# One gated cross-attention block with a mixture of experts: an expert product in front of the score maxima, stack copies in front of a scaling, loads with semaphores of their own, and the division of the expert weights moved into the first step

## The chip, the core and the metric

The kernel runs on 1 core of a Trainium2 chip. The core has a matrix engine (PE in the profile, with its weight loads as PEld), a vector engine (DVE), an activation engine (ACT), GpSimd (POOL) and a queue engine (SP) that issues the transfers between the chip's memory and the core's. The engines work through instruction lists of their own, each in order, and wait for each other by semaphores. The metric is the device time of one execution in microseconds. A step in this text is one pass of the kernel's outer loop, numbered from 0.

## The reference, cut to what matters

There are 32 rows (batch entries) of 256 tokens with 256 features, and for each row 77 context tokens with 192 features. A block of attention with 16 heads of 16 features and a two-layer product behind it is added to x through a gate, and then a mixture of 8 experts, of which 2 count for each token, through another.

```python
x = x + tanh(g_xattn) * xattn(layernorm(x), ctx)     # q, k, v with biases, softmax, relu(out @ W1 + b1) @ W2 + b2
x = x + tanh(g_ffn) * ffn(layernorm(x))

def ffn(x):                                          # E = 8 experts, K = 2
    scores = maximum(x @ gate_W + gate_b, 1e-4)
    p = softmax(scores)
    w = maximum(p, 0.1) at the top 2, divided by its sum; 0 elsewhere
    y = einsum('bsd,edf->bsef', x, expert_W) + expert_b
    return einsum('bsef,bse->bsf', y, w) / 2
```

## The kernel before

All weights stay in the core. Nearly every product is made three times, as high and low halves: a matrix is rounded to a high part (`we_hi`, `wkv_hi`, `w1_hi`, ...), usually by ACT, and what the rounding lost is the low part (`we_lo`, ...), usually made by DVE; PE then adds low x high, high x low and high x high. The expert weights are kept in float16 and are first divided by a power of two near their largest magnitude: DVE reduces `we_f` to `w_amax`, PE transposes it, DVE makes the power, PE spreads it over the partitions (`power_spread`), DVE makes `w_scale`, ACT makes `we_hi` (`experts_high`) and DVE `we_lo` (`experts_low`, four parts and a fifth piece for the gate weights and expert biases).

The outer loop is written by hand as a pipeline over rows: step s holds the front of row s (norm, keys, values, queries, score maxima, stacks), the middle of row s - 1 (`scores`, exponentials `exps`, `attend`, the two-layer product, second norm), the first experts of row s - 2 and the last experts of row s - 3. There are 35 steps; rows 0 to 31 have their front in steps 0 to 31. Each engine has its own `step` function, and the order of the calls there is the order of its instructions. Nothing reorders them.

Places that the change and the prediction touch:

- The maxima: `scores_for_max(b, i)` (line 845) are six products of the queries with `k_block`, a block form of the keys that POOL makes in two halves (`key_blocks(b, 0)` and `(b, 1)`, line 426). Product 0 waits for the first half, product 1 for the second. Between the halves POOL does `stack_comb` (three kinds of small copies). DVE reduces each product (`take_max`).
- The experts: `experts(e, eu, i, ...)` is one product of six matmuls of 512 columns (line 711, tile `e`), in two PSUM banks in turn. Products 2 and 3 are scaled by ACT (`scale_expert`, line 621), the other six are scaled and added by DVE (line 1156).
- The query stacks: PE transposes `q_stack` in two halves (line 911), ACT copies them (`qs_copy_a`, `qs_copy_b`, lines 602 and 606). The next step's `transposes_x` (line 720) writes the bank that `qs_copy_b` reads. ACT then goes on with `x2T_high` (612), `xnT_high` (522) and the first exponentials (544, 545); DVE makes `p_lo` from these (1139) and PE's first `attend` (780) reads it.
- The start: SP issues all transfers; nine of them share the semaphore `first_loaded`, which ACT and DVE await in whole. ACT runs `experts_high` in step 1, between its stack copies and `oT_high` (line 582), for whose low half `oT_lo` PE's `mlp_up` waits. DVE runs `experts_low` in step 1, among the maxima and `h_low` (line 1234, for `mlp_down`, line 894) and ahead of the second norm (`xn`, line 1254, for line 921).

Of the kernel before, what the change touches and what calls it, by code (L numbers as in the profile page):

```python
# [16 lines left out]
F32 = mybir.dt.float32  # L17
# [3 lines left out]
ALU = mybir.AluOpType  # L21
# [40 lines left out]
def gated_block(nc, x, y, g_xattn, g_ffn, Wq, bq, Wk, bk, Wv, bv, W1, b1, W2, b2,  # L62
# [5 lines left out]
    with ExitStack() as ctx:  # L68
# [29 lines left out]
        w_amax, w_top, w_power = sb("w_amax", [P, 2]), sb("w_top", [2, 1]), sb("w_power", [2, 1])  # L98
# [73 lines left out]
        first_loaded = sem("first_loaded")  # L172
        w_loaded = sem("w_loaded")
        we_loaded = sem("we_loaded")
# [4 lines left out]
        tanh_ready, b2g_ready = sem("tanh_ready"), sem("b2g_ready")  # L179
# [44 lines left out]
        FIRST, WEIGHTS = 9, 8  # L224
# [44 lines left out]
        def _(sp):  # L269
# [22 lines left out]
            for dst, src in [(wq_f[:], Wq.rearrange("(k p) n -> p k n", p=P)),  # L292
                             (wkv_f[:, :, 0:D], Wk.rearrange("(k p) n -> p k n", p=YC)),
                             (wkv_f[:, :, D:2 * D], Wv.rearrange("(k p) n -> p k n", p=YC)),
                             (bq_rows[:], bq.partition_broadcast(P)),
                             (bkv_rows[:, 0:D], bk.partition_broadcast(M)),
                             (bkv_rows[:, D:2 * D], bv.partition_broadcast(M)),
                             (gates[:, 0:1], g_xattn.partition_broadcast(P)),
                             (gates[:, 1:2], g_ffn.partition_broadcast(P)),
                             (b2_rows[:], b2.partition_broadcast(P))]:  # L300
                sp.dma_start(dst, src).then_inc(first_loaded, 16)
            sp.wait_ge(consts_ready, EARLY)
            for dst, src in [(w1_f[:], W1.rearrange("(k p) n -> p k n", p=P)),
                             (w2_f[:], W2.rearrange("(k p) n -> p k n", p=P)),
                             (gb_rows[:], gate_b.partition_broadcast(P)),
                             (gw_f[:], gate_W.rearrange("(k p) n -> p k n", p=P)),
# [5 lines left out]
            load(0, 1, 1)  # L312
            for k in range(KC):
                sp.dma_start(we_f[:, k, :].rearrange("p (e f) -> p e f", e=E),
                             expert_W[:, k * P:(k + 1) * P, :].rearrange("e p f -> p e f")).then_inc(we_loaded, 16)
# [6 lines left out]
        def _(pool):  # L322
# [121 lines left out]
            pool.wait_ge(b2g_ready, 1)  # L444
            x_with_bias(0, 0)

            def step(pair, u, s):
# [21 lines left out]
                if has(s, 0):  # L469
                    q_low(b)  # L470
                    v_parts(b, u)
                if has(s, 1) and s > 0:
                    first_norm_scale(n)
# [994 lines left out]
```

## Time and profile before

| what | value |
|---|---|
| time, median of 3 runs | 1013.13 us (1012.97 to 1013.41) |
| the profiled execution's own time | 1012.68 us |
| its span, first to last instruction | 1011.0 us |
| PE busy | 945.1 us, 93% |
| DVE, ACT, POOL busy | 82%, 71%, 64% |
| steps 0, 1 and 2 begin with line 720 at | 7.0, 34.6 and 75.4 us |
| a step in the middle | 29.5 us |

PE is busy nearly all the time from step 3 on; the profile's share counts overlapping ends of matmuls, so small waits show as less idle time than they cost. The first three steps are less dense. A row's start, its duration, the engine, the line and the tiles are read from left to right; what stands in square brackets is how long the engine was idle before it and what ended that.

### The profile page before, as it was taken

To read this page: it belongs to the slowest core of one execution; us is meant where nothing else is said; L and a number is where in the kernel's file an instruction comes from. 1 tells how busy PE (TensorE), PEld (TensorE's weight loads), DVE (VectorE), ACT (ScalarE), POOL (GpSimd) and SP (SyncE) were. 2 spreads that over 40 slices of the span, in tenths; PEclk is the share of its full clock that TensorE was granted. 3 is DMA by queue.
4 is the path that set the end of the run, shared out by engine and by line. 5 is a ranking of instruction groups with operands and counts; after the bars stand their busy time and mean duration, and the time that the engine had idled before them with its cause. 6 is when DMAs were issued, how large, how long until landed. Compare 5 with 4: busy or idle time off the path is not lost.

```text
span 1011.0 us, 26189 instructions
## 1 busy us (share of the span) xinstructions
PE 945.1 (93%) x9410; PEld 692.7 (69%) x9410; DVE 824.9 (82%) x2134; ACT 721.1 (71%) x1517; POOL 651.8 (64%) x856
## 2 busy tenths in 40 slices
PE   2758999999999999999999999999999999999997
PEld 2546677777767777776777777677777777777763
DVE  3566888888888888888888888888888888888875
ACT  4556787777778777777877777787777778777661
POOL 4435566777666677766667776666777666677643
PEclk9977999999999999999999999999999999999999
DMA  6000000000000000000000000000000000000000
GB/s 207 14 11 4 15 24 25 25 22 15 25 15 25 24 25 22 15 25 15 25 24 25 22 15 24 14 25 25 25 23 15 25 14 25 25 12 11 12 13 21
DMA packets 17472, 24.62 MB, mean 24 GB/s; under 512 B 2798, under 2 KB 8896, under 8 KB 17344
## 3 DMA queue, kind: packets, MB, share of 16 engines
q1 hardware_dynamic: 17344, 22.94, 7.1%
q8 instruction: 77, 1.26, 0.5%
q14 instruction: 51, 0.42, 0.1%
HBM read 14.54 MB, written 8.39 MB: 23 GB/s over the span
## 4 chain that ended last, share of the span: by engine, by line
PE 68%; POOL 11%; ACT 9%; issue 7%; DVE 3%; DMA 1%; SPq 0%; POOLq 0%; DVEq 0%; ACTq 0%
PE e L711 21%; PE g L711 20%; PE t L894 9%; POOL p_lo L372 6%; POOL k_block L426 5%; PE t L760 5%; PE s L845 4%; ACT qsT L606 3%; ACT scaled L621 2%; PE g L720 2%; ACT p_hi L545 2%; PE s L780 1%; PE g L856 1%; PE s L781 1%; PE s L782 1%
## 5 line engine op out<-in xcount | busy, mean ns | idle before, releaser
L372 POOL TENSOR_TENSOR p_lo<-p_f,p_hi 77x512 f16<-77x512 f32 x160 | 183.2, 1161 | 234.3 <-ACT p_hi L545 234.3
L711 PE MATMUL e<-we_hi,x2T_lo 128*128 128x512 f16 x496 | 188.9, 381 | 0.0
L711 PE MATMUL e<-we_hi,x2T_hi 128*128 128x512 f16 x496 | 188.4, 380 | 0.0
L711 PE MATMUL e<-we_lo,x2T_hi 128*128 128x512 f16 x496 | 188.4, 380 | 0.0
L544 ACT ACTIVATE p_f<-t 77x512 f32<-77x512 f32 x256 | 151.9, 593 | 24.8 <-PE t L760 24.4
L1156 DVE SCALAR_TENSOR_TENSOR acc<-e,comb,acc 128x256 f32<-128x256 f32 x307 | 145.9, 475 | 14.1 <-PE e L711 11.8
L545 ACT ACTIVATE p_hi<-t 77x512 f16<-77x512 f32 x256 | 151.9, 593 | 0.0
L1201 DVE TENSOR_REDUCE row_max<-s 128x6 f32<-128x462 f32 (+1 forms) x192 | 108.0, 576 | 11.4 <-PE s L845 11.4
L780 PEld LDWEIGHTS s<-v_hi,p_lo 77*128 77x128 f16 x1024 | 83.3, 96 | 32.2 <-issue 19.5
L780 PE MATMUL s<-v_hi,p_lo 77*128 77x17 f16 x1024 | 97.8, 172 | 5.2 <-POOL p_lo L372 2.5
L426 POOL TENSOR_TENSOR k_block<-own_head,khT 128x616 f16<-128x616 f16 x64 | 95.1, 1488 | 5.7 <-ACT khT L575 5.7
L621 ACT ACTIVATE scaled<-e,comb 128x256 f32<-128x256 f32 x126 | 53.0, 472 | 61.8 <-PE e L711 61.8
L782 PE MATMUL s<-v_hi,p_hi 77*128 77x17 f16 x1024 | 96.4, 170 | 0.0
L781 PE MATMUL s<-v_lo,p_hi 77*128 77x17 f16 x1024 | 96.3, 171 | 0.0
L760 PE MATMUL t<-qsT,kz 128*77 128x256 f16 x512 | 91.6, 282 | 2.8 <-ACT p_hi L545 2.5
L711 PEld LDWEIGHTS e<-we_hi,x2T_hi 128*128 128x128 f16 x496 | 48.5, 98 | 58.9 <-issue 0.6
L781 PEld LDWEIGHTS s<-v_lo,p_hi 77*128 77x128 f16 x1024 | 82.4, 96 | 7.1
L711 PE MATMUL g<-oT_hi,w_lo 128*128 128x256 f32 x256 | 80.8, 316 | 4.0 <-DVE oT_lo L1227 4.0
L845 PE MATMUL s<-k_block,qhT 128*128 128x308 f16 (+2 forms) x256 | 67.2, 307 | 16.4 <-POOL k_block L426 14.5
L590 ACT ACTIVATE h_hi<-g,b_cols 128x256 fp32r<-128x256 f32 x128 | 60.9, 476 | 29.4 <-PE g L711 27.6
L782 PEld LDWEIGHTS s<-v_hi,p_hi 77*128 77x128 f16 x1024 | 81.5, 96 | 0.0
L1139 DVE TENSOR_TENSOR p_lo<-p_f,p_hi 77x512 f16<-77x512 f32 x96 | 69.5, 724 | 13.6 <-ACT p_hi L545 13.6
(189 smaller groups left out, 2924.0 us busy)
## 6 DMA issues: line engine op xcount, KB each, us to landing
x_sb<-in_x SPq DMA_DIRECT2D x32, 256.0 KB, 2.6
out<-acc SPq DMA_DIRECT2D x32, 256.0 KB, 2.0
we_f<-in_L_ffn_expert_W SPq DMA_DIRECT2D x2, 1024.0 KB, 9.2
y_sb<-in_ctx SPq DMA_DIRECT2D x32, 57.8 KB
w_f<-in_L_xattn_W SPq DMA_DIRECT2D x2, 512.0 KB
wq_f<-in_L_xattn_Wq SPq DMA_DIRECT2D x1, 256.0 KB
wkv_f<-in_L_xattn_Wk SPq DMA_DIRECT2D x1, 192.0 KB
wkv_f<-in_L_xattn_Wv SPq DMA_DIRECT2D x1, 192.0 KB
```

The costliest lines, as they stand in the source:

```text
L372: pool.tensor_tensor(p_lo[:, r].rearrange("m h n -> m (h n)"), p_f[:, r, :], p_hi[:, r].rearrange("m h n -> m (h n)"), ALU.subtract).then_ ...
L426: pool.tensor_tensor(k_block[:, c * PAIRS:(c + 1) * PAIRS, :], own_head[:], khT[:, c, :].unsqueeze(1).to_broadcast([P, PAIRS, M]), ALU.mul ...
L544: act.activation(p_f[:, r, :], TT[g % 2][0:M, :], ACT.Exp, scale=SCALE).then_inc(exps_done, 1)
L545: act.activation(p_hi[:, r].rearrange("m h n -> m (h n)"), TT[g % 2][0:M, :], ACT.Exp, scale=SCALE).then_inc(exps_done, 1)
L711: mm = pe.matmul(out_ap, a, c, start=(i == 0), stop=(i == n - 1))
L760: mm = pe.matmul(TT[g % 2][0:M, e * N:(e + 1) * N], kz[:, g, e, :], qsT[:, g, :], start=True, stop=True)
L780: pe.matmul(dst, lo, v_hi[:, u, h, :], start=True, stop=False)
L781: pe.matmul(dst, hi, v_lo[:, u, h, :], start=False, stop=False)
L782: mm = pe.matmul(dst, hi, v_hi[:, u, h, :], start=False, stop=True)
L845: mm = pe.matmul(S[i % 2][:, at * M:(at + n) * M], qhT[:, h // PAIRS, t * P:(t + 1) * P], k_block[:, h:h + n, :], start=True, stop=True)
L1156: dve.scalar_tensor_tensor(out=acc[:, u, t, :], in0=BANK[product_banks(r)[i]][:, j * D:(j + 1) * D], scalar=comb[:, u, t, 2 * c + j:2 * c ...
L1201: dve.tensor_reduce(row_max[:, t, h:h + n], S[i % 2][:, 0:n * M].rearrange("p (h m) -> p h m", h=n), AX.X, ALU.max).then_inc(max_taken, 1)
```

## The change

1. PE: `experts(e, eu, 0, ...)` stands in front of `scores_for_max(b, 0)` instead of behind it (30 steps, 2 to 31, have both).
2. ACT: `qs_copy_a` and `qs_copy_b` stand in front of the second `scale_expert` (product 3) instead of behind it (the same 30 steps).
3. SP: the loads come in another order and with own semaphores: keys and values first, then the query weights, biases, the second row, the gates, the 2 MB of expert weights, and only then the two-layer weights. ACT and DVE wait for what they read.
4. The division of the expert weights is moved from steps 0 and 1 into step 0: the reduction is split over the two loads, the transposes, the power and the scales stand between the keys and the maxima of row 0, `experts_high` (ACT) and the first `experts_low` (DVE) end in step 0, and the other four pieces of `experts_low` are spread over step 1. The rounding of the two-layer weights goes to the end of step 0.

```diff
@@ SP @@
-            for dst, src in [(wq_f[:], ...), (wkv_f[:, :, 0:D], ...), (wkv_f[:, :, D:2 * D], ...), (bq_rows[:], ...),
...
-                sp.dma_start(dst, src).then_inc(first_loaded, 16)
+            sp.dma_start(wkv_f[:, :, 0:D], Wk.rearrange("(k p) n -> p k n", p=YC)).then_inc(kv_loaded, 16)
+            sp.dma_start(wkv_f[:, :, D:2 * D], Wv.rearrange("(k p) n -> p k n", p=YC)).then_inc(kv_loaded, 16)
+            sp.dma_start(wq_f[:], Wq.rearrange("(k p) n -> p k n", p=P)).then_inc(wq_loaded, 16)
...
+            load(0, 1, 1)
+            sp.dma_start(gates[:, 0:1], g_xattn.partition_broadcast(P)).then_inc(gates_loaded, 16)
+            sp.dma_start(gates[:, 1:2], g_ffn.partition_broadcast(P)).then_inc(gates_loaded, 16)
+            for k in range(KC):
+                sp.dma_start(we_f[:, k, :].rearrange("p (e f) -> p e f", e=E),
+                             expert_W[:, k * P:(k + 1) * P, :].rearrange("e p f -> p e f")).then_inc(we_loaded[k], 16)
             sp.wait_ge(consts_ready, EARLY)
+            sp.dma_start(gw_f[:], gate_W.rearrange("(k p) n -> p k n", p=P)).then_inc(gw_loaded, 16)
             for dst, src in [(w1_f[:], W1.rearrange("(k p) n -> p k n", p=P)),
                              (w2_f[:], W2.rearrange("(k p) n -> p k n", p=P)),
...
@@ ACT @@
-            act.wait_ge(first_loaded, 16 * FIRST)
-            act.activation(tanh_g[:], gates[:], ACT.Tanh).then_inc(tanh_ready, 1)
-            for hi, full in ((wkv_hi, wkv_f), (wq_hi, wq_f)):
-                act.activation(hi[:], full[:], ACT.Copy).then_inc(w_hi_ready, 1)
+            act.wait_ge(kv_loaded, 32)
+            act.activation(wkv_hi[:], wkv_f[:], ACT.Copy).then_inc(w_hi_ready, 1)
...
                     highT_copies(b)
                     q_stack_high(b)
                     k_stack_high(b)
-                if s == 1:
-                    experts_high()
+                if s == 0:
+                    weights_high()
+                    experts_high((0, 1))
...
                 if front:
                     kz_copy(b)
+                if s == 0:
+                    experts_high((2, 3))
+                    gate_and_biases_high()
...
-                if first:
-                    scale_expert(e, eu, 3, s - 2)
                 if front:
                     qs_copy_a(b)
                     qs_copy_b(b)
+                if first:
+                    scale_expert(e, eu, 3, s - 2)
                 if mid:
                     x2T_high(m, mu)
@@ PE @@
-                if s == 1:
-                    largest_weight_transposed()
...
-                if s == 1:
-                    power_spread()
...
+                if first:
+                    experts(e, eu, 0, s - 2)
+                if s == 0:
+                    largest_weight_transposed()
                 if front:
                     scores_for_max(b, 0)
-                if first:
-                    experts(e, eu, 0, s - 2)
+                if s == 0:
+                    power_spread()
@@ DVE @@
                 if front:
                     q_high(b)
                 if s == 0:
-                    weights_low()
+                    largest_expert_weights(0)
+                    largest_expert_weights(1)
+                    largest_weights()
+                    gate_factors()
+                    power_of_largest()
+                if s == 1:
+                    experts_low(2)
...
+                if s == 0:
+                    weight_scales()
                 if front:
                     take_max(b, 1)
                     take_max(b, 2)
                     kz_copy(b)
-                if s == 1:
-                    experts_low(0)
...
-                if s == 1:
-                    experts_low(2)
...
                 if s == 1:
-                    experts_low(3)
                     experts_low(PARTS)
...
                 if s == 0:
-                    largest_weights()
+                    weights_low()
+                    experts_low(0)
```

On PE, at the place in a middle step where the last of the products of `p` with the values (`s1<-v_hi,p_hi`) gives way to the maxima of the next row, this stood before (the line numbers of the two kernels differ; the three rows of tile e0, the expert product, stand twice in a row and are shown once):

```order
L782 MATMUL s1<-v_hi,p_hi 128x17
L845 MATMUL s0<-k_block,qhT 128x462
L711 MATMUL e0<-we_hi,x2T_lo 128x512
L711 MATMUL e0<-we_lo,x2T_hi 128x512
L711 MATMUL e0<-we_hi,x2T_hi 128x512
L856 MATMUL g0<-ident32,o 128x128 x4
L790 MATMUL g1<-ident32,comb_stack 96x128 x2
L845 MATMUL s1<-k_block,qhT 128x154
```

and this stands there now:

```order
L802 MATMUL s1<-v_hi,p_hi 128x17
L731 MATMUL e0<-we_hi,x2T_lo 128x512
L731 MATMUL e0<-we_lo,x2T_hi 128x512
L731 MATMUL e0<-we_hi,x2T_hi 128x512
L865 MATMUL s0<-k_block,qhT 128x462
L876 MATMUL g0<-ident32,o 128x128 x4
L810 MATMUL g1<-ident32,comb_stack 96x128 x2
L865 MATMUL s1<-k_block,qhT 128x154
```

The six expert matmuls and the first product with `k_block` changed places; from the output transposes (`g0<-ident32,o`) on, to the first product with the second half of `k_block` (128x154), the order is as before.

On ACT, at the end of a middle step, this stood before:

```order
L490 ACTIVATE xn<-x_sb,neg_mean 128x256 x2
L494 ACTIVATE xn<-xn,rstd 128x256 x2
L621 ACTIVATE scaled<-e,comb 128x256 x2
L602 ACTIVATE qsT<-g 128x1024
L606 ACTIVATE qsT<-g 128x1024
L612 ACTIVATE x2T_hi<-g 128x512
L522 ACTIVATE xnT_hi<-g 128x512
```

and this stands there now:

```order
L492 ACTIVATE xn<-x_sb,neg_mean 128x256 x2
L496 ACTIVATE xn<-xn,rstd 128x256 x2
L612 ACTIVATE qsT<-g 128x1024
L616 ACTIVATE qsT<-g 128x1024
L631 ACTIVATE scaled<-e,comb 128x256 x2
L622 ACTIVATE x2T_hi<-g 128x512
L532 ACTIVATE xnT_hi<-g 128x512
```

The two scalings moved behind the two stack copies, and stand now between these and the copies that open the next step (`x2T_hi`, `xnT_hi`).

On ACT in the first two steps, the part of step 0 behind the key stack reads now as follows (before, `kz` followed `k_stack` directly, `w_hi` stood ahead of the second row's norm, and `we_hi`, `gw_hi` and `eb_stack` stood in step 1 ahead of `oT_hi`):

```order
L568 ACTIVATE k_stack<-k_hi 77x32x16
L514 ACTIVATE w_hi<-w_f 128x1024 x2
L520 ACTIVATE we_hi<-we_f,w_scale 128x2x512 x2
L608 ACTIVATE kz<-t 64x8x77
L520 ACTIVATE we_hi<-we_f,w_scale 128x2x512 x2
L524 ACTIVATE gw_hi<-gw_f,w_scale 128x16
L527 ACTIVATE eb_stack<-eb_f,w_scale 32x256 x2
L612 ACTIVATE qsT<-g 128x1024
```

Everything that turns loaded weights into high parts stands now ahead of row 0's stack copies `qsT`, and nothing of it is left in step 1.

## Rows read from the trace of the kernel before

**Rows 1.** PE's waits: us in total, times, the longest in us

```profile
PE s L845 <- POOL k_block L426: 14.5, 31, 2.7
PE g L720 <- ACT qsT L606: 7.8, 30, 1.3
```

**Rows 2.** Step 2 and a middle step: stretch, length, busy PE PEld DVE ACT POOL, PEclk, DMA

```profile
75.40:109.20 33.80, 30.71 (x278) 22.11 (x276) 22.26 (x60) 22.27 (x48) 16.03 (x23) 0.83 0.04 10
404.00:433.40 29.40, 28.76 (x294) 21.16 (x295) 25.08 (x67) 22.14 (x48) 20.17 (x26) 1.00 0.07 22
```

**Rows 3.** Timeline of a middle step around the maxima; start, duration, engine

```profile
417.13 0.35 PE L845 MATMUL s<-k_block,qhT 128*128 128x462 f16 x1 [0.38 <-POOL k_block L426]
...
419.27 0.36 PE L845 MATMUL s<-k_block,qhT 128*128 128x154 f16 x2
...
415.33 1.70 POOL L426 TENSOR_TENSOR k_block<-own_head,khT 128x616 f16<-128x616 f16 x1
...
417.81 1.26 POOL L426 TENSOR_TENSOR k_block<-own_head,khT 128x616 f16<-128x616 f16 x1
...
415.11 0.80 DVE L1139 TENSOR_TENSOR p_lo<-p_f,p_hi 77x512 f16<-77x512 f32 x1
```

**Rows 4.** Timeline of that step's end and the next one's start, PE and ACT

```profile
430.41 1.06 PE L911 MATMUL g<-ident,q_stack 128*128 128x128 f16 x16
...
433.43 0.63 PE L720 MATMUL g<-ident,xn 128*128 128x128 f32 x4 [0.22 <-ACT qsT L606]
...
436.52 0.17 PE L780 MATMUL s<-v_hi,p_lo 77*128 77x17 f16 x1
...
430.62 0.84 ACT L621 ACTIVATE scaled<-e,comb 128x256 f32<-128x256 f32 x2 [1.88 <-PE e L711]
431.34 1.02 ACT L602 ACTIVATE qsT<-g 128x1024 f16<-128x1024 f16 x1
432.25 1.03 ACT L606 ACTIVATE qsT<-g 128x1024 f16<-128x1024 f16 x1
433.24 0.60 ACT L612 ACTIVATE x2T_hi<-g 128x512 f16<-128x512 f32 x1
434.09 0.60 ACT L522 ACTIVATE xnT_hi<-g 128x512 fp32r<-128x512 f32 x1 [0.25 <-PE g L720]
```

**Rows 5.** Timeline of step 0, and the start of step 1 (the last row)

```profile
10.80 0.20 ACT L499 ACTIVATE tanh_g<-gates 128x2 f32<-128x2 f32 x1 [3.91 <-DMA b_rows<-in_L_xattn_b]
...
15.54 0.68 PE L711 MATMUL g<-wkv_hi,yT_lo 96*77 96x512 f32 x1 [7.16 <-DVE yT_lo L1133]
...
21.67 0.43 DVE L1176 CAST q_hi<-q 128x512 f16<-128x512 f32 x1
...
34.58 1.09 PE L720 MATMUL g<-ident,xn 128*128 128x128 f32 x4 [1.27 <-ACT qsT L606]
```

**Rows 6.** The tile we_f: count, ns min/median/max, first and last start in us

```profile
L512 ACT ACTIVATE we_hi<-we_f,w_scale x4: 1164/1171/1179, 51.3 to 54.4; 128x1024 f16<-128x1024 f32 x4
L1123 DVE SCALAR_TENSOR_TENSOR we_lo<-we_f,w_scale,we_hi x4: 1275/1280/2377, 59.5 to 69.2; 128x1024 f16<-128x1024 f32 x4
L314 SPq DMA_DIRECT2D we_f<-in_L_ffn_expert_W x2: 373/1074/1774, 11.4 to 11.8; - x2
L1088 DVE TENSOR_REDUCE w_amax<-we_f x1: 4412/4412/4412, 31.0 to 31.0; 128x1 f32<-128x4096 f32 x1
...
DMA to landing us min/median/max: 8.0/9.2/10.4
```

**Rows 7.** Timeline of step 1 where PE waits for ACT or DVE

```profile
56.72 0.60 ACT L582 ACTIVATE oT_hi<-g 128x512 fp32r<-128x512 f32 x1
...
58.09 0.58 PE L711 MATMUL g<-oT_hi,w_lo 128*128 128x256 f32 x1 [4.04 <-DVE oT_lo L1227]
...
67.69 0.38 PE L894 MATMUL t<-w_hi,h_lo 128*128 128x256 f32 x1 [2.01 <-DVE h_lo L1234]
...
73.91 0.66 PE L921 MATMUL g<-ident,xn 128*128 128x128 f32 x2 [3.25 <-DVE xn L1254]
```

More of the change, by code:

```diff
@@ L97, in gated_block @@
         gb_rows = sb("gb_rows", [P, E])
-        w_amax, w_top, w_power = sb("w_amax", [P, 2]), sb("w_top", [2, 1]), sb("w_power", [2, 1])
+        w_amax, w_top, w_power = sb("w_amax", [P, 3]), sb("w_top", [2, 1]), sb("w_power", [2, 1])
         w_spread = sb("w_spread", [2, P])
@@ L496, in _, with query_weights_high, gate_tanh @@
             first_norm(0, 0)
[L498 to L501 removed]
+            act.wait_ge(kv_loaded, 32)
+            act.activation(wkv_hi[:], wkv_f[:], ACT.Copy).then_inc(w_hi_ready, 1)
+            def query_weights_high():
+                act.wait_ge(wq_loaded, 16)
+                act.activation(wq_hi[:], wq_f[:], ACT.Copy).then_inc(w_hi_ready, 1)
+            def gate_tanh():
+                act.wait_ge(gates_loaded, 32)
+                act.activation(tanh_g[:], gates[:], ACT.Tanh).then_inc(tanh_ready, 1)
             def weights_high():
@@ L506, in weights_high, with experts_high @@
                     act.activation(hi[:], full[:], ACT.Copy).then_inc(w_hi_ready, 1)
-            def experts_high():
+            def experts_high(parts):
                 act.wait_ge(w_scale_done, 1)
-                for i in range(PARTS):
+                for i in parts:
                     cols = slice(i * E * D // PARTS, (i + 1) * E * D // PARTS)
@@ L734, in largest_weight_transposed @@
             def largest_weight_transposed():
-                pe.wait_ge(w_amax_done, 2)
-                pe.transpose(BANK["e0"][0:2, 0:P], w_amax[:], ident32[:]).then_inc(w_amaxT_in_psum, 1)
+                pe.wait_ge(w_amax_done, 4)
+                pe.transpose(BANK["e0"][0:2, 0:P], w_amax[:, 0:2], ident32[:]).then_inc(w_amaxT_in_psum, 1)
             def power_spread():
@@ L1068, in _, with key_value_weights_low, query_weights_low, gate_factors @@
             first_norm_sums(0)
-            dve.wait_ge(first_loaded, 16 * FIRST)
-            dve.wait_ge(tanh_ready, 1)
-            dve.tensor_scalar(b2g_rows[:], b2_rows[:], tanh_g[:, 0:1], None, ALU.mult).then_inc(b2g_ready, 1)
-            dve.tensor_scalar(ffn_scale[:], tanh_g[:, 1:2], 1.0 / TOP_K, None, ALU.mult).then_inc(b2g_ready, 1)
-            for i, (lo, hi, full) in enumerate(((wkv_lo, wkv_hi, wkv_f), (wq_lo, wq_hi, wq_f))):
-                dve.wait_ge(w_hi_ready, i + 1)
-                dve.tensor_tensor(lo[:], full[:], hi[:].bitcast(F32), ALU.subtract).then_inc(w_lo_ready, 1)
-            dve.wait_ge(b2g_ready, 2)
+            def key_value_weights_low():
+                dve.wait_ge(w_hi_ready, 1)
+                dve.tensor_tensor(wkv_lo[:], wkv_f[:], wkv_hi[:].bitcast(F32), ALU.subtract).then_inc(w_lo_ready, 1)
+            def query_weights_low():
+                dve.wait_ge(w_hi_ready, 2)
+                dve.tensor_tensor(wq_lo[:], wq_f[:], wq_hi[:].bitcast(F32), ALU.subtract).then_inc(w_lo_ready, 1)
+                dve.wait_ge(consts_ready, CONSTS)
+                dve.wait_ge(rows_loaded, 48)
+            def gate_factors():
+                dve.wait_ge(tanh_ready, 1)
+                dve.tensor_scalar(ffn_scale[:], tanh_g[:, 1:2], 1.0 / TOP_K, None, ALU.mult).then_inc(ffn_scale_ready, 1)
             def weights_low():
-                dve.wait_ge(consts_ready, CONSTS)
                 dve.wait_ge(w_loaded, 16 * WEIGHTS)
+                dve.tensor_scalar(b2g_rows[:], b2_rows[:], tanh_g[:, 0:1], None, ALU.mult).then_inc(b2g_ready, 1)
                 for i, (lo, hi, full) in enumerate(((w1_lo, w1_hi, w1_f), (w2_lo, w2_hi, w2_f))):
```

72 lines of the change are left out of this document (40 added, 32 removed).

## The prediction

> **What bounds the kernel now.** I read the shares by engine, then PE's waits, then single steps. PE sets the pace: its idle time is a few short waits per step. The largest in sum is that of the maxima for `k_block` [rows 1]: 14.5 us over 31 times, 2.7 of them in step 0, so (14.5 - 2.7) / 30 = 0.39 us in each later step. Then comes that of `transposes_x` for the second stack copy, 7.8 us, 1.3 of them at the start of step 1 [rows 1, 5], so (7.8 - 1.3) / 29 = 0.22 us a step. The change stands in front of just these two. A step in the middle lasts 29.4 us from one `transposes_x` to the next, and step 2 lasts 33.8 us at a mean granted clock of 0.83 [rows 2]: it alternates between 1.2 and 2.4 GHz. From step 3 on the clock is up. Steps 0 and 1 are no steady pipeline: step 1 begins at 34.58 us [rows 5], and in it PE idles 4.04, 2.01 and 3.25 us for three products that wait on ACT or DVE [rows 7]. So there are two sums to make: thirty nearly equal steps, and the start.
>
> **Steady steps, the expert product in front of the maxima.** It removes nothing. Six matmuls that stood behind product 0 of the maxima now fill PE's time until the first half of `k_block` is there. That half ends at 415.33 + 1.70 = 417.03 and PE starts 0.10 later, at 417.13 [rows 3]. With the expert product ahead, PE has no wait there. But what is late next is the second half, in the same POOL queue behind `stack_comb`: it ends at 417.81 + 1.26 = 419.07. Product 1 stands behind the same work as before, and started at 419.27 [rows 3], 0.20 after the half was ready; of that 0.10 is the hop just measured. Nothing in the change makes POOL earlier: its chain begins with `khT` and with `p_lo`, which hang on PE's and ACT's earlier part of the step. So product 1 can start at 419.07 + 0.10 = 419.17 at the earliest. The wait of 0.39 us goes from product 0 to product 1, and **0.10 us a step** is left as gain. The output transposes and `oT_low` come earlier by the whole wait, but they are not what PE awaits next. I take 29 steps (3 to 31): -2.9 us. The bounds: 0 if the hop to product 1 is slower by 0.1, and 0.39 x 29 = 11.3 us if POOL does come earlier.
>
> The length of the second half matters, since it now ends the wait. The first half takes 1.70 and the second 1.26 us; beside the first runs DVE's `p_lo`, which itself takes 0.80 [rows 3]. If the second took 1.70 as well, product 1 would start 0.44 later and the step would be 0.44 - 0.10 = 0.34 us longer, not 0.10 shorter; the sum takes 1.26, since POOL does that half at the same time as before and DVE's order beside it is the same but for a shift of some tenths. The Trainium skill, GPSIMD Engine Reference, section 1, says that GpSimd shares its SBUF interfaces with VectorE and contends with DVE instructions that read two SBUF tensors. The trace agrees: the slow half is the one beside `p_lo`, which reads two. By that rule the second half keeps its 1.26, as long as nothing of that kind comes beside it, and the sum is the same.
>
> **Steady steps, the stack copies in front of the scaling.** ACT's order was scaling 430.62, copies 431.34 and 432.25, `x2T_hi` 433.24, `xnT_hi` 434.09 [rows 4]. The copies can't simply move up by the scaling's 0.72: the first needs eight of the sixteen transposes that begin at 430.41 and take 1.06 [rows 4], so it is ready at about 430.41 + 1.06 / 2 + 0.1 = 431.05. It starts 0.29 earlier, the second at 431.96, and, with the old hop of 433.43 - 432.25 - 1.03 = 0.15, PE's `transposes_x` at 431.96 + 1.03 + 0.15 = 433.14 instead of 433.43. But the scaling then stands between the copies and `x2T_hi`: 431.05 + 0.91 + 0.91 = 432.87, two scalings 0.72, `x2T_hi` at 433.6, `xnT_hi` half a microsecond later at 434.1, against 434.09 before. From there ACT goes without a gap to the first exponentials, DVE's `p_lo` and PE's first `attend` at 436.52 [rows 4], and PE waits there for whatever it gained. So the price is **0 to +0.04 us a step**; I take +0.02 x 29 = +0.6 us. Bounds: the 0.22 of [rows 1] in full, -6.4 us, if `attend` does not hang on ACT; and, if the copies came no earlier at all, 0.29 more a step, +8.4. Behind the later scaling wait the bank of product 3 for the last row's product 5, a step later, and POOL's `add_scaled`, later still; both have time.
>
> **Step 0.** ACT stood idle 3.91 us up to 10.80 for the last of nine loads [rows 5], so it was free at 6.89. Keys and values stand now right behind the first row in SP's queue and have a semaphore of their own, and I take them as landed by then. Each microsecond that they were later would be one on this chain. So `wkv_hi` begins 4.0 us earlier, and the low query half no longer stands ahead of the first product: keys start at about 10.9 instead of 15.54, and `q_hi`, which ended at 21.67 + 0.43 = 22.10, ends at about 17.5 [rows 5]. Then come the new parts. The reduction of the expert weights takes 4.41 us [rows 6] in two halves, to about 22. The loads must be there: they were issued at 11.4 and 11.8 and landed 8.0 and 10.4 us later [rows 6], at 19.4 and 22.2, behind 1 MB of other weights; now they are issued about 5 us earlier and ahead of that megabyte, so I put them at 14 to 18, ahead of their halves. Power, spread and scale are ten short instructions on DVE and PE; I bound them by 1.5 and 3 us and take 2.3: scales at 24.3. ACT's block is long: from the first `we_hi` at 51.3 to `oT_hi` at 56.72 it took 5.4 us [rows 6, 7], and with `kz` in it, which I put at 0.7, 6.1; so it ends at about 30.5. In that time lie the six maxima and the stack transposes, which are the cover on DVE and PE. Then come the two copies, 1.02 + 0.91 (as in [rows 4]), and step 1 starts at about 32.6 instead of 34.58 [rows 5]: **-2.0 us**. Ahead of the block ACT rounds the two-layer weights, which are now loaded last. All loads had landed by 11.8 + 10.4 = 22.2 [rows 6], the bytes are the same, and two roundings of about 1.1 us (estimate, from 1.17 for the same shape, [rows 6]) end at 24.4, just when the scales come: no cover is left there, and each microsecond that these loads are later is one on the path. Bounds: -2.8 and +0.5.
>
> **Step 1.** Without ACT's block `oT_hi` comes right behind the output transposes, and of the 4.04 us some 0.35 stay, the time of the copy and its low half: -3.7. `h_lo` was late because a part of `we_lo` stood ahead of it (2.38 us, the longest of the four, [rows 6]); the parts are moved into DVE's idle time earlier in the step, and -2.0 follows [rows 7]. The fourth part (1.28) no longer stands ahead of the second norm, the fifth piece does: -1.2 of the 3.25 [rows 6, 7]. Against that, the moved parts run beside POOL's `p_lo`, and such a part took up to 1.1 us longer than the others [rows 6]: +0.3, bounds 0 and +2.2. Together **-6.6 us** (-7.3 to -4.4).
>
> **Step 2.** It begins with the same idle stretch ahead of it, only shorter, so I expect it to start at 1.2 GHz again; but denser work should bring the clock up a little sooner: **-1.0 us**, bounds 0 and 33.8 - 29.4 = 4.4 [rows 2].
>
> The last three steps are unchanged. The sum: -2.0 - 6.6 - 1.0 - 2.9 + 0.6 = -11.9 us. On the profiled execution's 1012.68 (span 1011.0 and 1.7 around it) that is 1000.8 us; the median of the runs shown is 0.45 above that execution, within the steps' rounding.
>
> **The rivals.**
> *Both steady waits vanish.* Then 0.61 us a step go, 17.7 us, in place of 2.3: 985 us. For it: the rows name just these waits. Against it: the 0.20 us at product 1, and the unbroken ACT chain. 7%.
> *The clock stays up.* If the shorter stalls of step 1 don't let it fall, step 2 takes a middle step's time: another -3.4, 997.4 us. Against it: 2 us of idling are left of the 3.25 ahead of step 2. 12%. The Trainium skill, TensorE: Matmul & The Clock Gate, part 1, says that the throttled state is the default and activity releases it, which speaks for this; the trace agrees, with 0.83 in step 2 and 1.00 in the denser step [rows 2].
> *Loads bind step 0.* If the expert or two-layer weights land 4 to 6 us later than reckoned, the moved division waits in the middle of step 0, ACT with it, and its gain turns to +2 to +4: 1005 to 1007 us. 7%.
> *The second half of `k_block` slows to 1.70.* +0.34 x 29 = +9.9 in place of -2.9: 1013.6, no change. 3%.
> *ACT becomes the bound, slower than before.* If the scaling's whole 0.84 [rows 4] is added between the copies and `xnT_hi`, because the copies wait for the transposes anyway, a step grows by up to 0.84: +24.4 in place of +0.6, 1024.6 us. It decides from (2.0 + 6.6 + 1.0 + 2.9) / 29 = 0.43 us a step on. Against it: the half of the transposes is done 0.29 ahead of the old start of the copies. 4%.
>
> **How the numbers follow.** The forecast case has 67%. I predict 1000.8 us; the range of 993 to 1008 holds it with its unknown costs, the warm step 2 and the late loads, and leaves out the first rival and the last two, 14%, and some tails. Faster by over 0.2% (2 us, about what a measurement here can tell): 93%. Within: 3%. Slower: 4%.
>
> **What would show it.** PE's wait for `k_block` stays near 0.4 us a step, but in front of the 154-column product; a step lasts 29.3 to 29.5 us; `transposes_x` waits less and the first `attend` more. Step 1 begins near 32.6, step 2 near 66 us, and no wait of over 1 us for `oT_lo` or `h_lo` is left. A step under 29 us, or ACT idle while PE waits for `w_amax` or for loads in step 0, would make me wrong.

## The result and the profile after

The changed kernel takes 1005.78 us (median of 4 runs, 1004.77 to 1007.32), the kernel before, run beside it, 1013.05 us: the ratio is 0.993, with a 95% interval of 0.991 to 0.995. The forecast was 1000.8 us in a range of 993 to 1008. The sign and the range held; of the 11.9 us that the sum promised, some 7 came.

The waits of PE after, in us in total, times and longest, answer to [rows 1]:

```profile
PE g L740 <- ACT xn L496: 7.1, 1, 7.1
PE s L865 <- POOL k_block L427: 6.3, 29, 0.2
PE s L800 <- DVE p_lo L1174: 5.0, 4, 4.2
PE e L756 <- DVE w_amax L1123: 4.7, 1, 4.7
PE g L941 <- DVE xn L1289: 2.8, 2, 2.2
PE s L800 <- POOL p_lo L373: 2.7, 5, 0.7
```

The first row is the start of the program. The wait for `k_block` fell from 14.5 to 6.3 us, that of the steady `transposes_x` for `qsT` is gone, as are, in this execution, those for `oT_lo` and `h_lo` of step 1 [rows 7]. A new one came: 4.2 us, once, for DVE's `p_lo`. Next, steps 1, 2 and a middle one (stretch, length, busy PE PEld DVE ACT POOL, PEclk, which is the granted share of TensorE's 2.4 GHz, DMA share and GB/s), to be held against [rows 2]:

```profile
32.40:68.70 36.30, 25.93 (x230) 20.92 (x231) 26.68 (x47) 19.22 (x39) 16.34 (x20) 0.84 0.09 23
68.70:101.90 33.20, 30.96 (x278) 22.96 (x277) 22.06 (x59) 21.58 (x46) 16.00 (x23) 0.81 0.03 11
396.20:425.60 29.40, 29.00 (x295) 21.21 (x294) 25.21 (x67) 21.93 (x48) 20.16 (x26) 1.00 0.08 22
```

The starts of `transposes_x` in the two traces, stretch by stretch, say where the time went:

| stretch | before | after | difference | forecast |
|---|---|---|---|---|
| to step 1 | 34.58 | 32.39 | -2.2 | -2.0 |
| step 1 | 40.85 | 36.32 | -4.5 | -6.6 |
| step 2 | 33.85 | 33.22 | -0.6 | -1.0 |
| steps 3 to 30, each | 29.467 | 29.430 | -0.04, -1.0 in all | -0.08, -2.3 in 29 steps |
| from step 31 to the end | 76.6 | 78.2 | +1.6 | 0 |

The columns add up to -6.8 (spans of 1011.0 and 1004.2 us). Three rows want a cause: step 1, the middle steps, the end.

**Step 1.** The timeline of the changed kernel there, DVE and then POOL (start, duration):

```profile
46.74 5.33 DVE L1174 TENSOR_TENSOR p_lo<-p_f,p_hi 77x512 f16<-77x512 f32 x1 [1.50 <-ACT p_hi L555]
...
44.85 2.51 POOL L373 TENSOR_TENSOR p_lo<-p_f,p_hi 77x512 f16<-77x512 f32 x2 [2.21 <-ACT p_hi L555]
47.33 2.46 POOL L427 TENSOR_TENSOR k_block<-own_head,khT 128x616 f16<-128x616 f16 x2
49.75 0.66 POOL L379 TENSOR_TENSOR k_stack<-kv,k_hi 77x256 f16<-77x256 f32 x1
50.38 1.14 POOL L385 TENSOR_TENSOR q_stack<-q,q_hi 128x512 f16<-128x512 f32 x1
51.47 0.86 POOL L419 CAST v_hi<-kv 77x256 f16<-77x256 f32 x1
```

DVE's difference, 0.80 us in a middle step [rows 3], takes 5.33. It ends at 52.07, 0.60 behind the start of POOL's cast, and that cast takes 0.86 where it takes 0.40 in the trace of before. Until then POOL went from one two-input instruction to the next without a gap. So DVE seems to be let in only where one of POOL's instructions begins, and then that one is held for it.

**The middle steps.** PE's rows around the maxima and ACT's at the step's end, then POOL's second half and DVE's `h_lo`:

```profile
411.65 0.37 PE L865 MATMUL s<-k_block,qhT 128*128 128x154 f16 x2 [0.22 <-POOL k_block L427]
...
422.92 1.06 PE L931 MATMUL g<-ident,q_stack 128*128 128x128 f16 x16
...
425.65 0.63 PE L740 MATMUL g<-ident,xn 128*128 128x128 f32 x4
...
423.57 1.02 ACT L612 ACTIVATE qsT<-g 128x1024 f16<-128x1024 f16 x1 [2.42 <-PE g L931]
424.49 1.02 ACT L616 ACTIVATE qsT<-g 128x1024 f16<-128x1024 f16 x1
425.39 0.84 ACT L631 ACTIVATE scaled<-e,comb 128x256 f32<-128x256 f32 x2
426.11 0.62 ACT L622 ACTIVATE x2T_hi<-g 128x512 f16<-128x512 f32 x1
426.58 0.63 ACT L532 ACTIVATE xnT_hi<-g 128x512 fp32r<-128x512 f32 x1
427.06 0.61 ACT L554 ACTIVATE p_f<-t 77x512 f32<-77x512 f32 x1
...
410.33 1.26 POOL L427 TENSOR_TENSOR k_block<-own_head,khT 128x616 f16<-128x616 f16 x1
...
417.08 1.04 DVE L1269 TENSOR_TENSOR h_lo<-h_f,h_hi 128x256 fp32r<-128x256 f32 x2
```

Count from the query stack's transposes. `transposes_x` follows 425.65 - 422.92 = 2.73 us later, where it was 3.02 [rows 4]: 0.29 won. But `xnT_hi` comes 426.58 - 422.92 = 3.66 later, against 3.68 [rows 4]. The gain is spent inside ACT's queue. At the maxima, the 154-column product starts 411.65 - (410.33 + 1.26) = 0.06 behind the second half of `k_block`, against 0.20 [rows 3]: 0.14 won. Yet from the end of that half to the next query stack transposes it is 422.92 - 411.59 = 11.33 us, and was 430.41 - 419.07 = 11.34 [rows 3, 4]. Two `h_lo` that took 0.95 together in the trace of before take 1.04, `mlp_down` gets its fourth chunk 0.09 later, and the matmuls right behind the wait lose 0.04. So the step looks like a ring, stack transposes, ACT, exponentials, both key halves on POOL, maxima, `h_lo`, `mlp_down` and round again, on which each edit wins at its place and loses the same a little further.

**The end.** Two stretches with the same work, of before (first fence) and after, with the same columns as above:

```profile
963.80:973.80 10.00, 8.54 (x112) 5.34 (x113) 9.10 (x20) 8.69 (x18) 5.88 (x7) 1.00 0.01 2
```

```profile
955.40:965.40 10.00, 8.36 (x89) 4.62 (x89) 8.89 (x21) 8.02 (x18) 5.62 (x5) 0.83 0.01 2
```

In the third step from the end PE has little to do and waits several times for ACT and POOL. There the granted clock stood at 1.2 GHz for about a third of the stretch in the changed kernel, (1 - 0.83) / 0.5, and not in the profiled execution of before. Not all of the 1.6 us is the clock's: 0.27 of it is the mark itself, since with the stack copies in front `transposes_x` of step 31 stands that much earlier against the work of ACT and POOL around it. The table counts the same 0.27 as a gain up to step 3.

### The profile page after: what moved, and what is told of

Same layout as the page of the kernel before. It is cut to its first block, busy times and chain, and to the rows that moved or that the text cites. A ratio compares the mean times of both kernels' runs of the same rounds, so it can differ in the third digit from the quotient of the medians.

```text
span 1004.2 us, 26188 instructions
## 1 busy us (share of the span) xinstructions
PE 952.2 (95%) x9410; PEld 692.0 (69%) x9410; DVE 833.8 (83%) x2136; ACT 714.3 (71%) x1517; POOL 652.1 (65%) x856
## 3 DMA queue, kind: packets, MB, share of 16 engines
q8 instruction: 77, 1.26, 0.5%
## 4 chain that ended last, share of the span: by engine, by line
PE 62%; POOL 16%; ACT 9%; issue 7%; DVE 4%; DMA 1%; SPq 1%; POOLq 0%; ACTq 0%; DVEq 0%
PE g L731 19%; PE e L731 16%; PE t L914 9%; POOL k_block L427 8%; POOL p_lo L373 6%; PE t L780 3%; PE s L865 3%; ACT p_hi L555 3%; PE g L931 2%; DVE p_lo L1174 2%; ACT qsT L616 2%; PE s L800 1%; ACT p_f L554 1%; DMA we_f<-in_L_ffn_expert_W 1%; PE s L801 1%
## 5 line engine op out<-in xcount | busy, mean ns | idle before, releaser
L554 ACT ACTIVATE p_f<-t 77x512 f32<-77x512 f32 x256 | 154.3, 603 | 26.3 <-PE t L780 25.9
L555 ACT ACTIVATE p_hi<-t 77x512 f16<-77x512 f32 x256 | 154.4, 603 | 0.0
L612 ACT ACTIVATE qsT<-g 128x1024 f16<-128x1024 f16 x32 | 32.7, 1023 | 76.0 <-PE g L931 76.0
L1174 DVE TENSOR_TENSOR p_lo<-p_f,p_hi 77x512 f16<-77x512 f32 x96 | 74.6, 777 | 9.3 <-ACT p_hi L555 5.2
L914 PE MATMUL t<-w_hi,h_lo 128*128 128x256 f32 x256 | 78.2, 305 | 0.5 <-issue 0.2
```

The source lines that it names most:

```text
L554: act.activation(p_f[:, r, :], TT[g % 2][0:M, :], ACT.Exp, scale=SCALE).then_inc(exps_done, 1)
L555: act.activation(p_hi[:, r].rearrange("m h n -> m (h n)"), TT[g % 2][0:M, :], ACT.Exp, scale=SCALE).then_inc(exps_done, 1)
L914: mm = pe.matmul(T_DOWN[t][:, 0:D], a[:, c, rows], w[:, c, :], start=(c == 0 and i == 0), stop=(c == HC - 1 and i == 2))
```

## The experiments

"Middle steps" is the mean of steps 3 to 30. Kernels with the same code in those steps differ by 0.02 us in it (29.430 to 29.450), so less than that is not resolved.

**Each steady edit alone,** on the kernel before:

```diff
-                if front:
-                    scores_for_max(b, 0)
                 if first:
                     experts(e, eu, 0, s - 2)
+                if front:
+                    scores_for_max(b, 0)
```

> The kernel before with one edit: TensorE issues the expert product in front of the first maxima product. Theory of a loop (the step is a ring: query_stack_transposes on PE, stack copies and exponentials on ACT, both k_block halves on POOL, maxima, mlp_down, again): PE reaches the 154-column product when the second k_block half lands, which is 0.14 us a step earlier than before, and h_low then runs beside POOL's q_low, is 0.09 us longer, and gives most of it back; the middle steps last 29.45 to 29.47 us (before 29.47), mlp_down starts its fourth chunk 0.09 us late. Rival (the prediction's sum): 0.10 us a step is kept, middle steps of 29.37. Total 1010 to 1013 by the theory, near 1010 by the rival.

```diff
-                if first:
-                    scale_expert(e, eu, 3, s - 2)
                 if front:
                     qs_copy_a(b)
                     qs_copy_b(b)
+                if first:
+                    scale_expert(e, eu, 3, s - 2)
```

> The kernel before with one edit: ACT makes the two stack copies in front of the scaling of expert product 3. Theory of a loop: transposes_x no longer waits for qsT, but x2T_hi, xnT_hi and the exponentials stand behind the scaling, and begin 4.14 us after query_stack_transposes where they began 4.17 after; the middle steps last 29.44 us. Rival (the prediction's sum): 0.00 to 0.04 us longer than before, 29.47 to 29.51. A second rival: the whole wait of 0.22 us of transposes_x is won, 29.25. Total about 1012 by the theory.

Middle steps of 29.463 and 29.454 us against 29.467: neither edit is worth anything that can be seen alone, and the rivals of 29.37 and 29.25 are out. The times, 1014.91 and 1015.43 us in one run each, lie above what was expected, but within the seven runs of the kernel before beside them, 1012.10 to 1015.74. In the first kernel PE's wait for `k_block` fell to 10.0 us, in the second that for `qsT` to 1.3: the waits went, the time stayed. The second kernel had a surprise that was not expected of it. Its start is that of before, and still its `p_low(7)` in step 1 took long:

```profile
48.73 3.35 DVE L1139 TENSOR_TENSOR p_lo<-p_f,p_hi 77x512 f16<-77x512 f32 x1 [2.44 <-ACT p_hi L545]
...
49.07 2.47 POOL L426 TENSOR_TENSOR k_block<-own_head,khT 128x616 f16<-128x616 f16 x2
51.50 1.12 POOL L378 TENSOR_TENSOR k_stack<-kv,k_hi 77x256 f16<-77x256 f32 x1
```

Here it ended at 52.08, 0.58 behind the start of `k_low`, which took 1.12 in place of 0.67. So the stall does not need the new start: the old one can have it too. It came in one of three profiles with the old start, and in all seven with the new one in which POOL was not made to wait for `p_low(7)`.

**The start alone, and the changed kernel again** (the first is the changed kernel with both edits above undone):

> The changed kernel with both steady edits undone (expert product behind the first maxima product, stack copies behind the scaling); the new start stays. Theory: step 1 begins at 32.4 us, lasts 36.3 with p_low(7) at 5.3 us on DVE, step 2 lasts 33.2, middle steps 29.47; 1.0 us above the changed kernel, near 1006.5. Rival (the steady edits are worth the prediction's 2.3 us): near 1008.

> The changed kernel again, as it is. Theory (DVE's two-input difference is held off by back-to-back two-input work of POOL, which the order of the start sets up): p_low(7) of step 1 takes 5.3 us again, PE waits 4.2 us for it, step 1 lasts 36.3. Rival (a chance of one execution): p_low(7) takes about 0.9 us and step 1 lasts 32 to 33, the time is near 1002. The short fall of TensorE's clock in step 32, which one profile of the changed kernel has and that of before has not, comes again if the program sets it, and not always if it is chance (1.3 to 1.7 us).

1005.84 us (ratio 0.992, 0.991 to 0.994) and 1006.34 (0.993, 0.991 to 0.995), run on the same chip: the whole gain that these runs can tell is the start's, and the 1.0 us that was expected between the two did not show. No run separates the start's two parts, the order of the loads and the moved division. Middle steps 29.457 and 29.433. The stall came in both, 4.46 and 4.48 us long, with PE waiting 3.1 us for it. It was shorter than 5.33 because DVE was let in one instruction of POOL earlier: this time `q_low` was the one that was held, 1.60 us in place of 1.15. In the second execution PE also waited 1.1 us for `h_lo` in step 1, which it had not done in the first of the same kernel.

The short fall of the clock near the end came in both as well. The steps there are in the first kernel those of before, and its end takes 77.81 us against 76.61: ACT runs level with the trace of before, to 0.02 us, until 36 us behind the start of step 31, and is 1.21 us late at 43 us; the clock fell at 34.87 and rose at 38.28. So the fall is worth 1.2 us. From step 31 to the end it takes 77.5 to 79.2 us in every other profile of this study, and all but one of them (the keys together, below) have that fall. The execution that the forecast was reckoned from, with 76.6, did not.

**What holds `p_low(7)` up.** First DVE begins it later, by a write to a scratch tile `nap`; then POOL leaves it a gap:

```diff
+                if s == 1:
+                    dve.wait_ge(exps_done, 16)
+                    dve.memset(nap[:], 0.0)
                 if mid:
                     p_low(m, 7)
```

> The changed kernel with one small write of DVE to a scratch tile in step 1, between the end of the exponentials and p_low(7), so that p_low(7) begins about 0.3 us later. Theory (the difference gets in only at the end of one of POOL's two-input instructions, and which one is a matter of phase): p_low(7) lasts about 0.55 us from the start of some POOL instruction on, and that one is 0.46 us longer than usual; a start 0.2 to 0.3 us ahead of the first k_block, as in the middle steps, gives 0.8 to 0.95 us, another phase gives 2 to 5 us. Rival (the length depends on what the start left behind on DVE or on late data): 4.5 to 5.3 us wherever it begins. Step 1 lasts 32.2 to 33 us in the first case, 35.5 to 36.3 in the last.

```diff
+                if s == 1:
+                    pool.wait_ge(p_lo_vector, len(VECTOR_LOW))
                 if has(s, 0):
                     key_blocks(b, 0)
```

> The changed kernel, with one wait more: in step 1 POOL begins the key blocks only when DVE has done p_low(7). Theory (POOL's back-to-back two-input work holds DVE off): p_low(7) ends about 0.55 us after POOL's second p_lo, 1.2 us at most, PE's wait of 3.1 to 4.2 us for it goes, step 1 lasts 32 to 33 us where it lasted 35.5 to 36.3, and the total is 3 to 4 us below the changed kernel, near 1003. Rival (something else is late by then, a load or the second norm): the wait moves, step 1 stays above 35.

The first is inconclusive on the phase: the exponentials ended earlier in that execution, so in spite of the write `p_low(7)` began 0.57 us ahead of the first `k_block`, about as in the first profile of the changed kernel (0.59), lost that start and the next two, and ended 0.58 behind the start of `q_low`, 4.21 us long. With 35.06 us for step 1 it lies between the two that were expected. The second decides. 1000.21 us, step 1 lasts 32.31, step 2 31.61, and the stall is gone (DVE, then POOL):

```profile
45.84 1.43 DVE L1176 TENSOR_TENSOR p_lo<-p_f,p_hi 77x512 f16<-77x512 f32 x1 [1.25 <-ACT p_hi L557]
...
43.94 2.77 POOL L373 TENSOR_TENSOR p_lo<-p_f,p_hi 77x512 f16<-77x512 f32 x2 [1.94 <-ACT p_hi L557]
47.34 2.47 POOL L427 TENSOR_TENSOR k_block<-own_head,khT 128x616 f16<-128x616 f16 x2 [0.63 <-DVE p_lo L1176]
```

DVE gets in at the end of POOL's second `p_lo`, 43.94 + 2.77 = 46.71, and is done 0.56 later. With a wait of 0.6 us on POOL, step 1 is 4.0 us shorter than in the first profile of the changed kernel. Another clock could do that too, but does not here. Steps 1 and 2 of the kernel with the start alone, which stalls (first fence), and of this one, with the columns of the step table:

```profile
32.26:68.47 36.21, 25.68 (x231) 20.78 (x232) 26.68 (x47) 19.22 (x39) 16.20 (x20) 0.71 0.07 20
68.47:101.36 32.89, 29.09 (x279) 21.06 (x277) 23.43 (x60) 22.13 (x48) 15.98 (x23) 0.90 0.04 11
```

```profile
31.76:64.07 32.31, 25.39 (x230) 20.46 (x231) 22.82 (x47) 19.25 (x39) 16.09 (x20) 0.71 0.08 24
64.07:95.68 31.61, 28.47 (x277) 21.52 (x277) 22.18 (x59) 21.62 (x46) 16.06 (x23) 0.92 0.04 11
```

At the same granted clock of 0.71, step 1 takes 36.21 with the stall and 32.31 without. Step 2 is 1.6 us shorter than in the changed kernel, but at 0.92 in place of 0.81, so that is not shown to be the stall's.

**The same in the middle steps?** `p_low(7)` in front of the additions of product 6:

```diff
+                if mid:
+                    p_low(m, 7)
                 if last:
                     add_expert(f_pair, f, fu, 6, 0, s - 3)
```

> The changed kernel, with DVE's p_low(7) ahead of the additions of expert product 6 in every step that has both, so that it begins some 0.5 us earlier, in the middle of POOL's last p_lo, while POOL goes on with k_block, the comb copies and the second k_block without a pause. Theory (which boundary it gets is a matter of phase): in the middle steps it can lose the first boundary, and then lasts 2 to 5 us, PE waits for it, and the step grows by up to 4 us (30 to 33). Rival (the stall belongs to step 1 alone): 1.2 to 1.4 us, the step stays at 29.4.

1049.97 us, middle steps of 30.98: the size is in the expected range, the place is not. `p_low(7)` came no earlier against POOL: DVE now stood idle 0.82 us for the exponentials and began it 0.23 us ahead of the first `k_block`, and it took 0.81 us where it takes 0.80. So its phase was not tried here. But since product 6 was added later, expert product 0 began 0.27 us later, when its bank came free, and what follows on PE and DVE with it, while `k_block` on POOL did not move. The second `h_lo` then took 0.87 us in place of 0.61, the fourth began 0.55 us later in the step than in the changed kernel, and POOL's `xb` 0.19 us earlier. That was enough for another two-input difference of DVE to meet another instruction of POOL (DVE, POOL, then PE):

```profile
391.82 0.81 DVE L1174 TENSOR_TENSOR p_lo<-p_f,p_hi 77x512 f16<-77x512 f32 x1 [0.82 <-ACT p_hi L555]
...
403.97 1.44 DVE L1269 TENSOR_TENSOR h_lo<-h_f,h_hi 128x256 fp32r<-128x256 f32 x1
...
392.05 1.70 POOL L427 TENSOR_TENSOR k_block<-own_head,khT 128x616 f16<-128x616 f16 x1
...
403.86 1.27 POOL L366 TENSOR_TENSOR xb<-x_sb,b2g_rows 128x512 f32<-128x512 f32 x1
...
405.47 0.39 PE L914 MATMUL t<-w_hi,h_lo 128*128 128x256 f32 x1 [1.09 <-DVE h_lo L1269]
```

The fourth `h_lo` begins 0.11 us behind `xb`, which ends at 405.13; it ends at 405.41 and takes 1.44 where it takes 0.43, in each step. To see whether this is the cause, POOL was made to wait for it:

```diff
+                if has(s, -1) and has(s, 1):
+                    pool.wait_ge(h_lo_done, 4 * m + 4)
                 if has(s, 1):
                     x_with_bias(n, nu)
```

> The kernel with the early p_low(7), whose steps last 30.98 us because the fourth h_low begins just behind POOL's xb and takes 1.44 us, with one wait more: POOL begins xb only when DVE has done all four h_low. Theory (POOL's two-input instruction holds DVE's off): the fourth h_low takes 0.43 us again, mlp_down's wait of 1.1 us goes, and the middle steps last 29.43 to 29.75, the 0.27 us that expert product 0 waits for its bank being all that is left; total 1006 to 1015. Rival (the shifted order of DVE itself makes h_low late): 30.5 or more, total above 1035.

1022.21 us, middle steps of 29.95:

```profile
425.76 0.41 DVE L1271 TENSOR_TENSOR h_lo<-h_f,h_hi 128x256 fp32r<-128x256 f32 x1
...
426.25 1.31 POOL L366 TENSOR_TENSOR xb<-x_sb,b2g_rows 128x512 f32<-128x512 f32 x1 [0.57 <-DVE h_lo L1271]
```

1.03 of the 1.55 us a step came back. That is 0.2 short of the expected range: the second `h_lo`, 0.87 us beside POOL's `v_lo` against 0.61 in the changed kernel, is still held, and mlp_down with it. So the cause is right for the fourth `h_lo`, and the sum had left the second one out.

**The ring.** The scaling of product 3 is cut in two (the last argument says which half), half of it where ACT stands idle for the transposes:

```diff
+                if first:
+                    scale_expert(e, eu, 3, s - 2, (0,))
                 if front:
                     qs_copy_a(b)
                     qs_copy_b(b)
                 if first:
-                    scale_expert(e, eu, 3, s - 2)
+                    scale_expert(e, eu, 3, s - 2, (1,))
```

> The changed kernel, with the scaling of expert product 3 cut in two: its first half in front of the stack copies, where ACT waits for query_stack_transposes anyway, its second half behind them. Theory of a loop (from query_stack_transposes to the exponentials the chain runs through ACT's queue: 4.14 us now, 4.17 before, 3.87 with the half): the middle steps last 29.16 us, 0.27 less, the total falls by 7 to 8 us to 998 to 999. Rival (PE or POOL is the bound already, and the waits only move): middle steps of 29.35 or more, total 1004 to 1006.

996.67 us (ratio 0.982, 0.980 to 0.984), middle steps of 29.150, on the forecast of the ring to 0.01. The total fell by 9.1 us against the result's 1005.78, more than the 7 to 8 expected; the kernel's four runs spread over 4.6 us (994.21 to 998.76), and where the rest comes from is open. PE's and ACT's rows there:

```profile
421.18 1.06 PE L933 MATMUL g<-ident,q_stack 128*128 128x128 f16 x16
...
421.82 1.02 ACT L612 ACTIVATE qsT<-g 128x1024 f16<-128x1024 f16 x1
422.74 1.02 ACT L616 ACTIVATE qsT<-g 128x1024 f16<-128x1024 f16 x1
423.65 0.48 ACT L631 ACTIVATE scaled<-e,comb 128x256 f32<-128x256 f32 x1
...
425.06 0.58 ACT L554 ACTIVATE p_f<-t 77x512 f32<-77x512 f32 x1
```

From the transposes to the first exponential it is 425.06 - 421.18 = 3.88 us, against 427.06 - 422.92 = 4.14 in the changed kernel; 0.26 less, and the step is 0.28 shorter. `qsT` starts as early as in the changed kernel, and only one scaling is left in front of `x2T_hi`.

**Both remedies,** and two variations on them: the second key half right behind the first on POOL, with the transposes of `comb` behind expert product 1 on PE; and the expert product back behind product 0 of the maxima.

> The changed kernel with both remedies: POOL begins step 1's key blocks only when DVE has done p_low(7), and the scaling of expert product 3 stands half in front of the stack copies and half behind them. Theory (two separate causes, in step 1 and in the middle steps): step 1 lasts 32.3 us, the middle steps 29.15, the total is the sum of both gains, 4 to 5.6 us below the halves alone: 991 to 993. Rival (the two overlap): 994 or more.

```diff
                 if has(s, 0):
                     key_blocks(b, 0)
+                    key_blocks(b, 1)
                 if has(s, -2):
                     stack_comb(e, eu)
                 if has(s, 0):
-                    key_blocks(b, 1)
                     k_low(b)
...
-                if first and s <= B:
-                    combT_transposes(e, eu)
                 if front:
                     scores_for_max(b, 1)
                 if first and s <= B:
                     experts(e, eu, 1, s - 2)
-                    expert_biases(e)
+                    combT_transposes(e, eu)
...
                 if front:
                     key_stack_transposes(b)
+                if first and s <= B:
+                    expert_biases(e)
```

> The kernel with both remedies, and POOL makes the second key half right behind the first, ahead of the four small comb instructions; TensorE transposes comb behind expert product 1 and adds the biases behind the key stack's transposes. Theory of a loop (PE's wait of 0.2 us for the second half, and 0.8 us of small POOL work ahead of it, lie on the ring): PE does not wait for k_block, the middle steps last 28.6 to 29.0, the total 979 to 988. Rival (the ring is not the only bound, another instruction of DVE is held off by POOL or mlp_down waits for h_lo): 29.1 or more, total 990 and up.

> The kernel with both remedies, with the expert product back behind the first maxima product. Theory (product first wins 0.14 us at the second key half, and DVE's h_low gives 0.09 to 0.13 of it back): middle steps of 29.15 to 29.20, total 991 to 994. Rival (the prediction's 0.10 us a step for product first, which only the late stack copies hid): 29.25, total 994 to 996.

With both remedies it is 993.47 us (ratio 0.980, 0.979 to 0.981), the fastest here; step 1 lasts 33.4 (32.3 expected), step 2 30.6, the middle steps 29.148. The median lies 0.5 above the expected range, 3.2 below that of the halves alone. The keys together failed: 1039.43 us (1.025, 1.024 to 1.027), middle steps of 30.70. PE's waits there:

```profile
PE t L918 <- DVE h_lo L1273: 27.8, 29, 1.0
PE e L735 <- DVE acc L1195: 14.3, 29, 0.5
```

The wait for `k_block` did go, but expert product 1 then waits 0.5 us for its bank, which DVE frees no earlier; `mlp_up` begins 0.54 us later in the step than with both remedies, since the transposes of `comb` and the biases now stand right in front of it; and that shift again puts the fourth `h_lo` 0.12 us behind the start of `xb`, where it takes 1.45. Three orders were changed at once here, and no run with `xb` held back was made of it. The last variation, 994.07 us, has middle steps of 29.185, so with the shorter ring the expert product in front is worth 0.04 us a step, little over what the traces resolve.

## Why the prediction was right, and where not

The sign and the range held, but the total is in part luck: the steady edits, for which -2.3 us was forecast, show as 0 to -1, and in step 1 two errors of opposite sign, each outside its bounds, cancel in part.

- **Step 0** held: -2.0 forecast, -2.2 and -2.4 in two profiles. The text said that ACT idle while PE waits for `w_amax` or for loads would make it wrong. Just that happened, 4.7 us on PE and 2.54 on ACT, and cost nothing: the scales came at 24.3 us, as reckoned, and ACT was done with the late two-layer weights just then. The sign to watch was badly chosen.
- **Step 1** has the term that was mis-sized: contention with POOL, "+0.3, bounds 0 and +2.2". It cost 3.9 us at equal clock (36.21 against 32.31 with the gap on POOL), and not on the moved parts of `we_lo`, but on `p_low(7)` behind them, which the change doesn't touch. The items that were to vanish did vanish (an `h_lo` wait of 1.1 us came back in some profiles), and without the stall the step is 8.5 us shorter than in the trace of before, more than the bound of -7.3. The bounds were also added up wrongly: from -3.7 - 2.0 - 1.2 and 0 to +2.2 they are -6.9 to -4.7, not -7.3 to -4.4.
- **Step 2:** -0.6, inside the bounds. It started at 1.2 GHz again, mean 0.81, so the rival of the warm clock did not come. Its length wanders with the clock: 33.22 and 34.59 in two profiles of the same kernel. In the kernels with the start alone and with both remedies it did start at 2.4 GHz, behind the same idle 2.15 us of PE, and took 32.89 and 30.62, not a middle step's time. Step 2 was to begin near 66 us and began at 68.71, late by the stall (64.07 with the gap on POOL).
- **Product first:** the mechanism was right. The wait moved to the 154-column product, which started 0.06 behind the second half; the sum had 0.10. The step that failed is "0.10 us a step is left as gain": it ended at that product and did not follow the step round to where the same POOL work is awaited again. The gain was 0 to 0.04. The sign that the wait would stay near 0.4 us a step did not fit the sum either, which left 0.39 - 0.10; it measured 6.3 / 29 = 0.22.
- **Copies first:** right in its numbers: `transposes_x` 0.29 earlier, `xnT_hi` where it was, price about nothing. The next question, how to take the scaling out of that chain, was not asked; its answer was worth 0.28 us a step.
- **"The last three steps are unchanged":** their code is, but from step 31 on they took 1.6 us more than in the one trace that was read, 1.2 of it since that one had escaped the fall of the clock.

The Trainium skill, SBUF — State Buffer, section "Who interferes with whom", says that a DVE instruction with two SBUF inputs contends with a GpSimd instruction that reads SBUF; its section "Summary: rules for kernel authors" adds that the second one to issue is blocked until the first is done. The fourth `h_lo` agrees with it, done 0.28 us behind `xb`. Step 1 does not quite: `p_low(7)` was kept out over up to five instructions of POOL, not one. The Trainium skill says, too, in "Who interferes with whom", that a DVE instruction with at most one SBUF input, outside a mode that takes both ports, does not contend. `oT_lo`, which reads PSUM and one SBUF tile, agrees: 0.69 us in every step of every profile, though POOL works beside it.

Open stays which of POOL's starts DVE gets. With 0.22 us to go it got the next one in the middle steps, with 0.34 to go it got it in step 1 of before (49.36 and 49.70) and lost it in step 1 of the kernel with the copies first (48.73 and 49.07). No run here told a rule for it.

## What to carry to other kernels

A wait that is removed is a gain only if the shift survives a full turn of the loop: follow it from the removed wait to the place where the same producer is awaited again, and look on the way for queues (here ACT's) into which the work was merely moved. Where DVE and POOL both read two SBUF tiles at a time, a small shift can cost much (here 0.27 us at its start, 1.55 us a step in the end); leave POOL a gap where DVE's result is awaited. Take the reference trace from more than one execution before a sum of single microseconds is built on it.

## What the hardware showed that was not expected

- A DVE difference of 0.7 to 0.9 us took 3.35 to 5.33 us in step 1 beside POOL work without a gap, in eight of ten profiles (one of them with the old start), and each time ended some 0.6 us behind the start of a POOL instruction that was itself about 0.46 us longer than elsewhere. In the four profiles in which POOL waited for it, it took 1.16 to 1.43 us.
- Moving one DVE instruction ahead of two others, with no work added, cost 44 us in all, by a shift against POOL that began as 0.27 us a step.
